# Mask added on TensorE and exponentials read from PSUM in steps 3 to 7 of iteration 1 of an attention and feed-forward kernel

## The reference

```python
q = layernorm(x) @ w_q.T        # 32 heads of 32
k = ctx @ w_k.T                 # 8 groups of 32, four heads share one
v = ctx @ w_v.T
scores = q . k / 32 ** 0.5      # per head, 128 x 128
scores = where(mask, scores, finfo.min)
x = x + (softmax(scores) @ v) @ w_out.T
h = layernorm(x) @ w12.T + b12  # 2048, in two halves
x = x + (silu(h1) * h2) @ w3.T + b3
```

## Time and profile before

| | us |
|---|---|
| median of three runs | 1041.63 |
| span of the profiled execution | 1040.4 |
| PE busy | 1017.7 (98%) |
| VectorE busy | 661.6 (64%) |
| ScalarE busy | 447.3 (43%) |
| GpSimd busy | 498.6 (48%) |
| ACT exponentials, L1153, 512 of them | 162.7 |
| DVE masking, L1820, 512 passes | 143.5 |

### The profile page before, as it was taken

One profiled execution on the slowest core, in us unless ns is written; L12 is line 12 of the kernel. 1 busy time (PEld: TensorE's weight loads), 2 busy tenths in 40 slices (PEclk: granted clock), 3 DMA queues, 4 the chain that ended last, 5 costly groups with the idle time before them and its releaser, 6 DMA issues.

```text
span 1040.4 us, 21876 instructions
## 1 busy us (share of the span) xinstructions
PE 1017.7 (98%) x8400; PEld 695.6 (67%) x8400; DVE 661.6 (64%) x2080; ACT 447.3 (43%) x983; POOL 498.6 (48%) x476
## 2 busy tenths in 40 slices
PE   7897999999999999999999999999999999999998
PEld 6786868869687696886655544444444888468853
DVE  6789977767787777888646234636864447625431
ACT  6768556557465574664766210123431112202100
POOL 2869923727337273379958596158742301212000
PEclk9999999999999999999999999999999999999999
DMA  9669686998989999789946715494758631974201
GB/s 367 227 160 197 168 216 168 222 247 222 248 211 229 230 245 244 179 236 232 268 94 123 253 71 203 94 345 160 272 200 185 235 112 40 236 230 122 83 31 51
DMA packets 230776, 199.12 MB, mean 191 GB/s; under 512 B 177040, under 2 KB 187280, under 8 KB 225808
## 3 DMA queue, kind: packets, MB, share of 16 engines
q1 hardware_dynamic: 230672, 197.72, 69.0%
HBM read 119.04 MB, written 35.65 MB: 149 GB/s over the span
## 4 chain that ended last, share of the span: by engine, by line
PE 87%; DVE 6%; DMA 1%; ACT 1%; issue 0%; SPq 0%; DVEq 0%
PE bank_dense L1349 52%; PE bank_spare L1349 13%; PE bank_score L1494 6%; PE bank_spare L1494 6%; PE bank_av L1494 3%; PE bank_score L1406 2%; DVE arena_attn L1820 2%; DVE arena_attn L1830 1%; PE bank_av L1424 1%; PE bank_av L1428 1%; PE bank_av L1426 1%; PE bank_dense L1366 1%; DMA k_scratch<-arena_in 1%; PE bank_spare L1358 0%; PE bank_dense L1358 0%
## 5 line engine op out<-in xcount | busy, mean ns | idle before, releaser
L1153 ACT ACTIVATE arena_attn<-arena_attn,arena_in 128x128 f32<-128x128 f32 x512 | 162.7, 391 | 94.6 <-DVE arena_in L1820 93.6
L1349 PE MATMUL bank_dense<-arena_rows,arena_in 128*128 128x256 f16 (+1 forms) x1272 | 175.2, 295 | 1.9 <-POOL arena_in L874 1.0
L936 POOL TENSOR_TENSOR arena_attn<-arena_attn 128x512 f16<-128x512 f32 x89 | 102.6, 1170 | 148.8 <-ACT arena_attn L1160 148.8
L1349 PE MATMUL bank_dense<-arena_attn,arena_rows 128*128 128x512 f16 x768 | 166.4, 379 | 0.0
L1349 PEld LDWEIGHTS bank_dense<-arena_rows,arena_in 128*128 128x128 f16 x1272 | 123.0, 98 | 43.1 <-DVE arena_in L1668 1.6
L1820 DVE CUSTOM_DVE_ANT_0 arena_attn<-bank_score,arena_in 128x128 f32<-128x128 f32 x512 | 143.5, 346 | 0.4 <-PE bank_score L1406 0.4
L1349 PEld LDWEIGHTS bank_dense<-arena_attn,arena_rows 128*128 128x128 f16 x768 | 75.2, 98 | 90.2
L1349 PE MATMUL bank_dense<-arena_out,arena_attn 128*128 128x512 f16 x576 | 127.8, 379 | 0.0
L1349 PEld LDWEIGHTS bank_dense<-arena_out,arena_attn 128*128 128x128 f16 x576 | 55.5, 98 | 63.3
L1349 PE MATMUL bank_spare<-arena_rows,arena_in 128*128 128x256 f16 (+1 forms) x648 | 87.6, 292 | 0.0
L1349 PE MATMUL bank_dense<-arena_out,arena_in 128*128 128x512 f16 x384 | 83.0, 379 | 0.0
(11 more groups left out here) (219 smaller groups left out, 1890.8 us busy)
## 6 DMA issues: line engine op xcount, KB each, us to landing
arena_rows<-x SPq DMA_DIRECT2D x32, 512.0 KB, 6.1
arena_in<-w_scratch SPq DMA_DIRECT2D x64, 256.0 KB, 3.1
arena_attn<-q_scratch SPq DMA_DIRECT2D x48, 256.0 KB, 4.5
arena_rows<-w_t SPq DMA_DIRECT2D x12, 1024.0 KB, 6.2
arena_rows<-ctx_t SPq DMA_DIRECT2D x8, 1024.0 KB, 6.1
q_scratch<-arena_attn SPq DMA_DIRECT2D x16, 512.0 KB, 5.1
x_scratch<-arena_rows SPq DMA_DIRECT2D x16, 512.0 KB, 3.8
arena_out<-x_scratch SPq DMA_DIRECT2D x16, 512.0 KB, 5.9
```

The costliest lines, as they stand in the source:

```text
L936: ins = pool.tensor_tensor(p_split[:, g % 2, u, 1], e[:, g % 2, u], p_split[:, g % 2, u, 0], ALU.subtract)
L1153: ins = act.activation(head, head, ACT.Exp, bias=neg_max[:, g % 2, h:h + 1], scale=-1.0)
L1349: ins = pe.matmul(dst, lhs(a, c), rhs(b, c), start=(c == chunks[0] and n == 0), stop=(c == chunks[-1] and n == 2))
```

## The change

For the units 3 to 7, all in iteration 1, the mask is added by PE: ahead of each head's score product a product of the identity with the mask, both in bfloat16, starts the accumulation, and the score product adds to it. VectorE's part becomes one maximum over the eight heads straight from PSUM (`raw_max`) and one small multiplication by `c_neg`, and it comes before the divide. The exponentials read the scores from PSUM and take the factor `c_pos = -c_neg` as their scale, in the same two halves as before. The next unit's score products therefore wait for the exponentials (`s_exp`). Three small operations are added ahead of it on VectorE.

```diff
+MASK_ON_PE = range(3, GROUPS)
 ...
 exps(g, u):
     act.wait_ge(s_neg, U * g + u + 1)
+    if g in MASK_ON_PE:
+        if g == MASK_ON_PE[0]:
+            act.wait_ge(s_c_pos, 1)
+        if g >= 2:
+            act.wait_ge(s_plo, plo_count(g - 2))
     for j in range(HPG):
-        ins = act.activation(head, head, ACT.Exp, bias=neg_max[:, g % 2, h:h + 1], scale=-1.0)
+        if g in MASK_ON_PE:
+            ins = act.activation(head, B_SCORE[:, SEQ * h:SEQ * h + SEQ], ACT.Exp,
+                                 bias=neg_max[:, g % 2, h:h + 1], scale=c_pos[:, g:g + 1])
+        else:
+            ins = act.activation(head, head, ACT.Exp, bias=neg_max[:, g % 2, h:h + 1], scale=-1.0)
 ...
 scores(g):
-    if g >= 1:
+    if g - 1 in MASK_ON_PE:
+        pe.wait_ge(s_exp, U * g)
+    elif g >= 1:
         pe.wait_ge(s_neg, U * g)
+    if g in MASK_ON_PE:
+        pe.wait_ge(s_mask_b, 2)
     for u in range(U):
         for j in range(HPG):
+            if g in MASK_ON_PE:
+                pe.matmul(B_SCORE[...], ident_b, mask_b, start=True, stop=False)
             ins = pe.matmul(B_SCORE[...], q_stack[...], k_stack[...],
-                            start=True, stop=True)
+                            start=g not in MASK_ON_PE, stop=True)
 ...
 block_scales(a):
+    if a == 0:
+        dve.tensor_scalar(c_pos, c_neg[:, 0], -1.0, None, ALU.mult).then_inc(s_c_pos, 1)
 ...
 mask_scores(g):
     dve.wait_ge(s_score, g + 1)
+    if g in MASK_ON_PE:
+        if g >= 2:
+            dve.wait_ge(s_exp, 2 * g - 2)
+        dve.tensor_reduce(raw_max, B_SCORE[:, :].rearrange("p (h n) -> p h n", n=SEQ), AX_X, ALU.max)\
+           .then_inc(s_raw_max, 1)
+        dve.wait_ge(s_raw_max, g + 1 - MASK_ON_PE[0])
+        dve.tensor_scalar(neg_max[:, g % 2], raw_max, c_neg[:, a % 2, m:m + 1], None, ALU.mult)\
+           .then_inc(s_neg, U)
+        return
 ...
 once, ahead of iteration 1:
+dve.tensor_scalar(mask_b, mask_u8[:, :], -1.0, -MASKED, ALU.add, ALU.mult).then_inc(s_mask_b, 1)
+dve.tensor_copy(ident_b, ident[:, :]).then_inc(s_mask_b, 1)
 ...
 in each step of the vector stream:
-    if g >= 3:
-        divide(g - 3)
-    mask_scores(g)
+    if g in MASK_ON_PE:
+        mask_scores(g)
+        divide(g - 3)
+    else:
+        if g >= 3:
+            divide(g - 3)
+        mask_scores(g)
```

More of the change, by code:

```diff
@@ L409, in xattn_ffn @@
         kept, with_6, with_5, with_7 = [terms[:, 0], terms[:, 1]], terms[:, 2], terms[:, 3], terms[:, 4]
+        ident_b = part(arena_attn, 59, 1, BF16)[:, 0:P]
+        mask_b = part(arena_attn, 59, 1, BF16)[:, P:2 * P]
+        c_pos = part(arena_attn, 59, 1, F32)[:, P:P + GROUPS]
+        raw_max = part(arena_attn, 59, 1, F32)[:, P + GROUPS:P + 2 * GROUPS]
         k_stack = part(arena_attn, 63, 4).rearrange("p (b g n) -> p b g n", b=2, g=4)
@@ L559, in xattn_ffn @@
         s_av, s_inv, s_avread = sem("av_done"), sem("inv_sum_done"), sem("attn_ready")
+        s_mask_b, s_raw_max, s_c_pos = sem("mask_for_pe_done"), sem("raw_max_done"), sem("c_pos_done")
         s_scales, s_cout = sem("block_scales_done"), sem("c_out_done")
@@ L1401, in scores @@
                     pe.wait_ge(s_kst[m // 4], STACKED * (a + 1))
-                if g >= 1:
+                if g - 1 in MASK_ON_PE:
+                    pe.wait_ge(s_exp, U * g)
+                elif g >= 1:
                     pe.wait_ge(s_neg, U * g)
+                if g in MASK_ON_PE:
+                    pe.wait_ge(s_mask_b, 2)
                 for u in range(U):
                     for j in range(HPG):
+                        if g in MASK_ON_PE:
+                            pe.matmul(B_SCORE[:, HALF * u + SEQ * j:HALF * u + SEQ * j + SEQ], ident_b, mask_b,
+                                      start=True, stop=False)
                         ins = pe.matmul(B_SCORE[:, HALF * u + SEQ * j:HALF * u + SEQ * j + SEQ],
```

## The result

The changed kernel is slower: 1046.39 us in the median of its runs (1045.14 to 1048.62) against 1042.01 for the kernel before beside it, ratio 1.0042 with a 95% interval of 1.0028 to 1.0057, so 4.4 us slower. Forecast were 3.4, with a range of 1041.6 to 1047.2.

A forecast was written before the change was run, and what follows sets the result against it. VectorE was taken to bound steps 3 to 7; its 3.6 us saving gives way to three loops of 6.60 us against 5.73, making V's read 3.4 late: 1041.63 + 3.4 = 1045.0 us, range 1041.6 to 1047.2.

The forecast's parts named there:

- the ring: Steps 3 to 7: scores, maxima, scaling, first exponentials, two high parts, second exponentials, next scores; 6.60 us against 5.73 now.
- price: Each exponential on ScalarE, reading PSUM with pointers for bias and factor, was taken 0.065 us longer than now.
- the term for GpSimd: VectorE's small scaling waits for a GpSimd instruction it meets: 0.32 us a step in the mean, bounds 0 and 0.84.
- The starts forecast for steps 4 to 7: Score products on PE were to start near 85.0, 91.6, 98.2 and 104.8, the last 3.35 us late.
- the first high part: ScalarE's high part of the projection, between the exponential halves; with that of the attention output it was given 0.53 us.
- it holds only instructions that follow each other by data or order: Said of the cheap 5.76 us cycle, against the rival that VectorE's relief comes through (1038.0 us, chance 0.07).
- The waits of 6.7 us go: PE's three waits for transposed probabilities in steps 3 to 8, 6.7 us in all, were to vanish.
- nothing gives this back: After VectorE's read of the V bank PE is dense, so its 3.4 us delay was to stay.
- Read of the V bank: VectorE's read after the scores of step 7, for which PE waits; forecast at 110.42, 3.4 us late.

The follow-up runs named there:

- const_factor: The changed kernel with a constant factor instead of the pointer in the exponentials, and another bias column; 0.8 us faster than the kernel before by the medians, 0.5 by the ratio.
- one_exp: The changed kernel with one maximum and one 512-column exponential for the four heads of each half; ratio 0.9991 to the kernel before, 0.9992 with the divide first.
- the price alone: The kernel before with a pointer for the factor in the exponentials of steps 3 to 7 and nothing else; ratio 1.0010.
- after_again: The changed kernel run once more, unaltered; ratio 1.0034 to the kernel before.
- before_again: The kernel before run once more, unaltered, for a second profile; ratio 1.0003.
- wait_alone: The kernel before with only the wait of the scores of steps 4 to 8 moved from the maxima to the exponentials; 1.6 us slower by the ratio.
- halves_all: The changed kernel with both exponential halves ahead of the high parts, maxima, scaling and scores by halves, and maxima 16 bytes apart; 1.2 us slower than before.
- filled: The changed kernel with six more 512-column matmuls ahead of the weighing of steps 3 to 6, their result overwritten; 3.4 us slower than the kernel before.
- halves_divide_first: halves_all with the old order on ScalarE and the divide ahead of the maxima; ratio 1.0016 to the kernel before.

## Why the prediction was right, point by point

**The mechanism is as forecast.** Scores wait for exponentials and VectorE idles for scores. That the length of the ring makes the loss is shown: with the wait kept and the exponentials shorter (const_factor, one_exp) no loss is left. How much wait and price make apart from each other is less sure: the wait alone costs 1.6 us (0.2 to 2.9), the price alone 1.0 (-0.5 to 2.7). Neither reaches the 4.4 measured, but their sum may.

**The ring's terms.** Step 5 at full clock is 1.14 (scores to maxima; forecast 1.23), 1.33 (1.24), 0.27 for a scaling that meets no GpSimd (0.27), 1.39 (1.43), 0.53 (0.53) and 1.59 (1.58): 6.25 against a forecast 6.28 without the term for GpSimd. The maxima took 1.225 us (1.21). Exponentials took 463 ns in the median (451), 74 more than before. Of these 74 the second pointer is 86 (463 against 377 in const_factor), and the PSUM source with one pointer saves 12 (389 against 377); by the shortest of each it is 90 (449 against 359) and 25 (384 against 359). The Trainium skill (ScalarE: Activation LUTs, What ACT_TABLE_LOAD costs, and VectorE: DVE Perf Modes, The TRN2 errata) made them 50 ns dearer than before, as an estimate, from 93 for the pointer and 43 saved by the source: the trace agrees with the first and not with the second. The matmuls of the mask hold up PE's next piece by 0.49 us more (0.93 instead of 0.44), where 0.44 was forecast.

**GpSimd.** Beyond 0.23 the scalings of steps 3 to 6 took 0, 0.44, 0 and 0.69, 0.28 in the mean, where 0.32 was forecast; the one at 103.59 ends with the GpSimd instruction, as the prediction said. In after_again they took 0.11, 0, 0.10 and 0.16, 0.09 in the mean, so the near hit of the first profile is luck.

**Missed: PE's clock.** The starts forecast for steps 4 to 7 were 85.0, 91.6, 98.2 and 104.8. Less the 2.3 of the start-up they were 84.95, 92.54, 98.79 and 106.33: 1.5 late in the end. That is the excess of the first high part over its 1.39 behind the first half in steps 4 and 6: 2.31 - 1.39 = 0.92 and 106.53 - 104.54 - 1.39 = 0.60. The ring had no term for the projection on PE, because it was done long before ScalarE asked for it at 2.78 us; at 4.45 us it was not. In after_again the fall in step 5 also slows the scores themselves: 1.72 us to the maxima instead of 1.14, and then 0.57 more at the first high part, 1.15 in all. The step that failed is "it holds only instructions that follow each other by data or order": the order on ScalarE lets PE's projection in, and PE's own pace was taken as fixed.

**Mis-sized: the transposes.** "The waits of 6.7 us go" held but for one of 1.9 us in step 3, whose DMA was issued at 78.90 and landed 7.7 us later. It cost little: the scores of step 4 start at 87.26, 0.2 behind the exponentials that they would have waited for.

**Failed: "nothing gives this back".** Read of the V bank forecast 31.9 us after the scores of step 3, measured 33.6. Then 1.1 us come back: steps 8 to 10 take 6.51 us each instead of 6.67, 6.66 and 7.34. In step 10 of the profile of before PE waited for the divide:

```profile
128.87 0.44 PE L1366 MATMUL bank_spare<-arena_in 128*128 128x128 f32 x2 [0.61 <-DVE arena_in L1838]
```

These 0.83 us of step 10 are not the change's: before_again has 6.67, 6.66 and 6.51. What the change gives back is the 0.3 of steps 8 and 9. It is the same wait, too short to be listed: before the change VectorE's divide ends 3.11 and 3.08 us after the scores' start and PE's turning begins 0.06 behind it, at 3.17 and 3.14; after it the divide ends at 2.61 and 1.97, and the turning begins at 3.07 and 3.06, behind PE's own work. It is not the new work that does it, since wait_alone has 6.50, 6.53 and 6.51 too, nor mere lateness, since halves_all, as late, has 6.70, 6.56 and 7.24. Why VectorE comes to these divides earlier stays open.

**The sum:** 3.4 forecast, 1.5 for the clock and 0.2 elsewhere more, 1.1 given back: 4.0, which is the difference in S0..S11 (76.09 - 72.06). Of the 1.1, though, 0.8 are the chance of that one profile of before; against before_again the difference is 5.0, and 4.3 between the means of the two profiles of each kernel. The timed 4.4 and 3.4 of the two comparisons lie on both sides of that. That the forecast was near is in part luck: the clock, for which it had no term, added 1.5 us in one profile. What stays open is how much of the loss the clock makes in the mean over executions; two profiles of the changed kernel have it in two steps and in one before step 7, and the timed runs at equal clocks say that most of the loss is not its second step.

## What to carry to other kernels

When an engine is relieved by letting a later reader use a shared buffer directly, write down the ring that the buffer's reuse closes, with every instruction that stands between its parts in any engine's order, and compare its length with today's step: 2.2 to 2.9 us saved on VectorE were worth nothing against a ring 0.5 us longer than the step. In such a ring each small price counts by its repeats (86 ns eight times), and the engines that seem to have room put their slow steps into the time too. Fewer and larger instructions on the ring took back the loss, and reordering them did not.

## What the runs showed of the hardware that I had not expected

- The granted clock of PE falls to 0.69 to 0.85 in single steps of 8 of the 14 profiles, one of the kernel before too, in other steps from execution to execution; 24 matmuls of 256 columns then take up to 4.45 us instead of 2.78. In const_factor, filled and both one_exp kernels, where PE waits less, the changed steps were all at 1.00; but halves_divide_first has 1.00 too, with 5.2 us of waits.
- The start-up has it as well (0.66 to 1.00 from 10 to 20 us), and the scores of step 0 start anywhere from 58.6 to 62.8 us, a scatter as large as what this change costs. In the timed runs of the kernel before, 0.001 less of mean granted clock goes with 0.5 to 1.0 us more.
- Writing the input of a small VectorE scaling 16 bytes apart did not keep it from waiting for GpSimd (0.43 us beside an instruction of 1.03, up to 1.04 us in halves_divide_first, 0.23 alone).
- A bf16 and an f16 matmul of 128 columns, alternating eight times, start 0.058 us apart, where eight of f16 alone take 0.055 each (0.44 us): the mixed types cost next to nothing beyond the columns.
